# Regional attention: the score maxima reach the query tile through TensorE instead of DRAM, with a lag of one step, and the loads are issued by SyncE

## The chip, the cores and the metric

The kernel runs on one core of one Trainium2 chip. The metric is the device time of one execution in microseconds. Loading the inputs to the device is not in it.

## The reference

The input has 32 images of 56 x 56 positions with 64 channels. A 3 x 3 convolution with quantized activations (8 levels) and one-bit weights comes first, then one transformer block:

```python
xq = round(min(1, abs(x)) * 7) / 7
x  = conv3x3(xq, sign(W) * mean(abs(W))) + b
# block; 7 x 7 regions of 8 x 8 = 64 tokens, 8 heads of 8 channels
q, k, v = split(layernorm(x) @ wqkv + bqkv)
idx  = top_k(mean_region(q) @ mean_region(k).T, 4)     # 4 regions for each region
attn = softmax(q_region @ k[idx].T / sqrt(8)); o = attn @ v[idx]
x = x + o @ wo + bo
x = x + gelu(layernorm(x) @ w1 + bm1) @ w2 + bm2
```

## The kernel before, in words

The images go in 16 pairs. One **step** is one region of one image: 98 steps a pair, 1568 in all. The program's `steps` runs steps 0 to 17 once, then a loop whose body is steps 18 to 115 (`LEAD`=18, `END`=116), so that the end of one pair overlaps the start of the next. Each engine has its own instruction list, written by hand as a function `step(p, h, kind)`, and the engines meet only in semaphores. An engine does its list strictly in that order.

What a step h does, with the lags `ST_LAG`=3 and `PV_LAG`=4:

- POOL and VectorE copy the keys of the four chosen regions into `kg` (`keys`), two steps ahead; POOL copies the values into `vg`.
- TensorE, `scores` (L988): four products of `qm` and `kg`, 256 columns each, into PSUM banks 0 and 1, queries on the rows. VectorE reduces them to the maximum of each query and head (L724) into `mx`. The scores of step h+1 overwrite these banks and so wait for it.
- VectorE transposes the maxima (L731) into `tr`. SyncE (SP) writes `tr` to DRAM as `max_d` (L370) and, one step later, reads it back as one row of `qm` (L364), row 96. `kg` has -1 in that row.
- TensorE, `turned(h-3)` (L1002): the same scores again with keys on the rows, in PSUM banks 2 and 3. Row 96 subtracts the maximum in the product. ScalarE takes the exponential of each bank (L832) into `pt`.
- TensorE, `attended(h-4)` (L1019): 32 small products of `pt` and `vg`, bank 4. ScalarE copies it to `um` (L837) at the end of a group of two steps (one at the seventh).

Between these, each engine has items of two other chains, spread over the steps by tables. `p_item`: the strips of the next pair (7 strips, one every 6 steps, from step 18, offsets 0 to 10): convolution (L881, offset 0), copy to `xi` on ScalarE (L762, offset 1) and centring, square (L765, 2) and variance, normalization (3), query and key products (4), value products (L901, 5), copies of the results by VectorE (L659 and L665), and stores to DRAM. `f_item`: finishing of this pair (7 strips, one every 7 steps, from step 60, offsets 0 to 13): softmax sums (L938, 0), their reciprocal by a logarithm and an exponential (1, 2), output product (4), second normalization (5 to 7), feed-forward products L969 (9) and L974 (10), and the two products back (12, 13). At offset 10 ScalarE runs `hidden` (L813): the Gelu table is loaded, four Gelus run, and the table of the other functions is loaded back (L199). L974 there waits for VectorE's copy of the first half (`z_ready`), which stands behind the step's reduction. `x_item` is the input of the pair after the next; ScalarE takes magnitudes (L781) when an image strip has landed.

In TensorE's `step`, the order before is scores, turned, attended, then strip and finishing items. In ScalarE's it is items, the two exponentials, the copy of `um`, the loads, and last `hidden`. The loads (`loads`: queries for the next seven steps, L237, and keys and values of a half, L247) are issued from ScalarE's queue.

## Time and profile before

| | |
|---|---|
| runs, us | 5547.73, 5552.67, 5535.24; median 5547.73 |
| profiled execution: span, us | 5568.0 |
| instructions in it | 230234 |
| busy: PE, VectorE, ScalarE, POOL | 84%, 62%, 59%, 49% |
| DMA | 487.33 MB in 627124 packets |

The profile is of one execution. Its span runs from the first to the last instruction; no time of that execution outside the span is shown. In it PE is TensorE's matmul, PEld its weight load, DVE VectorE, ACT ScalarE, POOL GpSimd, SP SyncE; a q behind a name is the engine's sequencer.
### The profile page before, as it was taken

To read this page: it belongs to the slowest core of one execution; us is meant where nothing else is said; L and a number is where in the kernel's file an instruction comes from. 1 tells how busy PE (TensorE), PEld (TensorE's weight loads), DVE (VectorE), ACT (ScalarE), POOL (GpSimd) and SP (SyncE) were. 2 spreads that over 40 slices of the span, in tenths; PEclk is the share of its full clock that TensorE was granted. 3 is DMA by queue.
4 is the path that set the end of the run, shared out by engine and by line. 5 is a ranking of instruction groups with operands and counts; after the bars stand their busy time and mean duration, and the time that the engine had idled before them with its cause. 6 is when DMAs were issued, how large, how long until landed. Compare 5 with 4: busy or idle time off the path is not lost.

```text
span 5568.0 us, 230234 instructions
## 1 busy us (share of the span) xinstructions
PE 4677.0 (84%) x68754; PEld 3217.0 (58%) x68754; DVE 3447.6 (62%) x7969; ACT 3285.4 (59%) x6282; POOL 2747.0 (49%) x9656
## 2 busy tenths in 40 slices
PE   2388888888889888888888888888888888888888
PEld 1265565656556565565656656565565656556564
DVE  2266666666666666666666666666566666667665
ACT  1156556565665656556565665656556565665656
POOL 1245455454544545445454554545455454554553
PEclk8589999998998999889989999989899999989999
DMA  1333343333333333333333423333343333323311
GB/s 53 102 98 92 83 109 76 100 77 96 102 77 98 84 95 91 82 103 80 94 83 91 111 72 103 81 96 92 79 109 79 96 81 102 100 75 102 84 40 33
DMA packets 627124, 487.33 MB, mean 88 GB/s; under 512 B 483792, under 2 KB 613968, under 8 KB 615536
## 3 DMA queue, kind: packets, MB, share of 16 engines
q10 hardware_dynamic: 335360, 205.62, 16.4%
q1 hardware_dynamic: 290416, 265.73, 16.2%
q8 instruction: 603, 9.88, 0.8%
q14 instruction: 745, 6.10, 0.4%
HBM read 262.38 MB, written 208.73 MB: 85 GB/s over the span
## 4 chain that ended last, share of the span: by engine, by line
PE 45%; DMA 18%; issue 10%; SPq 7%; ACT 7%; DVE 5%; DVEq 3%; POOL 2%; ACTq 2%; POOLq 1%
DMA max_d<-tr 11%; PE ps L988 9%; PE ps L1002 7%; PE ps L1019 7%; PE ps L881 4%; DMA qm<-qk_d 3%; PE ps L938 3%; DMA xin<-in_x 3%; DVEq L223 2%; DVE mx L724 2%; SPq L327 2%; PE ps L949 2%; PE ps L901 2%; ACT hid L813 2%; PE ps L974 2%
## 5 line engine op out<-in xcount | busy, mean ns | idle before, releaser
L724 DVE TENSOR_REDUCE mx<-ps 128x4 f32<-128x1024 f32 x1568 | 1921.7, 1226 | 1702.3 <-PE ps L988 1354.0
L832 ACT ACTIVATE pt<-ps 128x512 f32<-128x512 f32 x3136 | 1694.3, 592 | 869.2 <-PE ps L1002 814.4
L506 POOL COPY vg<-vs 64x64 f32 x6272 | 1526.5, 243 | 782.0 <-POOL kg L490 576.7
L988 PE MATMUL ps<-kg,qm 96*128 96x256 f32 x6272 | 1336.2, 338 | 386.6 <-DVE mx L724 127.3
L490 POOL CAST kg<-ks 96x128 fp32r x3136 | 851.0, 297 | 1511.6 <-PE ps L1002 1156.6
L988 PEld LDWEIGHTS ps<-kg,qm 96*128 96x128 f32 x6272 | 946.8, 202 | 1053.6 <-issue 889.5
L1002 PE MATMUL ps<-qm,kg 97*128 97x256 f32 x6272 | 1119.8, 301 | 178.8 <-ACT pt L832 102.3
L1019 PE MATMUL ps<-pt,vg 128*32 128x64 f32 x50176 | 1091.4, 231 | 0.0
L1002 PEld LDWEIGHTS ps<-qm,kg 97*128 97x128 f32 x6272 | 926.2, 203 | 252.2 <-ACT pt L832 164.8
L1019 PEld LDWEIGHTS ps<-pt,vg 128*32 128x32 f32 x50176 | 826.1, 115 | 224.2 <-issue 34.8
L643 DVE CAST kg<-ks 96x128 fp32r x3136 | 625.6, 241 | 126.2 <-issue 123.5
L518 POOL TENSOR_SCALAR xin<-xin 128x448 f32<-128x448 f32 x119 | 205.1, 1723 | 449.4 <-ACT xin L781 442.6
L731 DVE STREAM_TRANSPOSE tr<-mx 128x32 f32<-128x32 f32 x1568 | 314.7, 201 | 3.4 <-issue 3.1
L881 PE MATMUL ps<-xT,wconv 128*128 128x448 bf16 x1008 | 267.6, 413 | 11.5 <-POOL xT L528 11.5
L938 PE MATMUL ps<-um,pick 128*128 128x448 f32 x448 | 213.8, 603 | 55.9 <-DVE vstg L665 40.6
L837 ACT ACTIVATE um<-ps 128x128 f32<-128x128 f32 (+1 forms) x896 | 240.5, 268 | 30.8 <-PE ps L1019 29.6
L776 ACT ACTIVATE stg<-ps,made 128x448 fp32r<-128x448 f32 x224 | 141.9, 637 | 183.1 <-PE ps L897 94.5
L974 PE MATMUL ps<-nm,w 64*128 64x448 f32 x448 | 144.0, 726 | 124.0 <-DVE hid L710 123.9
L790 ACT ACTIVATE rc<-ps 128x448 f32<-128x448 f32 x224 | 121.7, 543 | 146.6 <-PE ps L938 85.3
L762 ACT ACTIVATE xi<-ps 128x448 fp32r<-128x448 f32 x112 | 61.1, 545 | 228.3 <-PE ps L881 228.3
L781 ACT ACTIVATE xin<-xin 128x448 f32<-128x448 f32 x119 | 68.6, 576 | 207.2 <-DMA xin<-in_x 199.2
L528 POOL TENSOR_SCALAR xT<-xin 128x448 bf16<-128x448 f32 x119 | 163.1, 1371 | 28.9 <-POOL vg L506 26.2
(109 smaller groups left out, 3866.7 us busy)
## 6 DMA issues: line engine op xcount, KB each, us to landing
qk_d<-stg SPq DMA_DIRECT2D x224, 448.0 KB
qm<-qk_d ACTq DMA_DIRECT2D x1792, 42.0 KB
ks<-qk_d ACTq DMA_DIRECT2D x96, 784.0 KB, 6.2
vs<-v_d ACTq DMA_DIRECT2D x64, 784.0 KB, 6.7
xin<-in_x SPq DMA_DIRECT2D x119, 224.0 KB
xi_d<-xi SPq DMA_DIRECT2D x112, 224.0 KB
qk_d<-stg SPq DMA_DIRECT2D x112, 224.0 KB
max_d<-tr SPq DMA_DIRECT2D x1568, 2.0 KB
```

Of the source, the lines that this page charges most:

```text
L490: j = pool.tensor_copy(kg[slot][0:NP3, :, 2 + k, :], ks[place(m)[0]][0:NP3, :, bass.ds(region, 1), :].rearrange("p g o t -> p g (o t)"))
L506: j = pool.tensor_copy(dst.rearrange("p j (e x) -> p j e x", e=2)[:, :, :, 0:HD], vs[place(m)[0]][rows, bass.ds(region, 1), :].rearrange(" ...
L643: j = v.tensor_copy(kg[slot][0:NP3, :, k, :], ks[place(m)[0]][0:NP3, :, bass.ds(region, 1), :].rearrange("p g o t -> p g (o t)"))
L724: v.tensor_reduce(mx[h % 2][:].rearrange("p (g j e) -> p g j e", g=2, j=2)[:, :, :, 0], ps[:, 0:2, :].rearrange("p g (j k) -> p g j k", j= ...
L731: v.transpose(tr[h % 2][:], mx[h % 2][:]).then_inc(S["tr_ready"], 1)
L832: act.activation(pt[m % 2][:, c], ps[:, 2 + c, :], ACT.Exp, scale=float(HD) ** -0.5).then_inc(S["pt_ready"], 1)
L881: i = pe.matmul(ps[:, 5, 0:ST].rearrange("p (n y c) -> p n y c", n=NW, y=WS), wconv[:, tap, :], rhs, start=tap == 0, stop=tap == 8)
L938: pe.matmul(ps[:, 5 + i, 0:ST], pick[:], src, start=True, stop=True).then_inc(S["sum_full"], 1)
L974: pe.matmul(ps[:, (7, 5)[i], 0:ST], w1[d, 128:256], nm2[d], start=True, stop=True).then_inc(S["h_full"], 1)
L988: i = pe.matmul(ps[:, g, 256 * j:256 * j + 256], qm[c % 2][0:NP3, t, g, 2 * j:2 * j + 2, :].rearrange("p h t -> p (h t)"), kg[slot][0:NP3, ...
L1002: i = pe.matmul(ps[:, 2 + b, 256 * g:256 * g + 256], kg[slot][0:NP3 + 1, g, 2 * b:2 * b + 2, :].rearrange("p k t -> p (k t)"), qm[c % 2][0 ...
L1019: i = pe.matmul(ps[32 * j:32 * j + 32, 4, RT * u:RT * u + RT], vg[slot][:, w:w + 32], pt[m % 2][:, c, n:n + RT], start=c + e == 0, stop=c ...
```

## The change

- The maxima stay on the chip. VectorE writes them to `mx` with 66 columns for each of two head pairs; all other columns are zero. TensorE multiplies each 66-column half as weights with an identity of 128 columns (new function `shifts`), which puts the maxima as rows into PSUM bank 2, at partitions 0 and 32. ScalarE copies 2 rows x 256 from partition 0 and VectorE 2 x 256 from partition 32 into rows 96 and 97 of `qm`. The turned product contracts over 98 rows instead of 97.
- The lags are 1 (turned), 2 (attended) and 3 (copy to `um`) instead of 3, 4 and 4. `turned` waits for both copies.
- TensorE's order in a step is now: products of the maxima of step h-1, scores h, strip and finishing items, turned h-1, attended h-2. The products of the maxima wait for the first exponential of step h-2, which frees bank 2.
- ScalarE's step begins with its copy, and the copy to `um` stands before the exponentials. VectorE's step ends with its copy.
- The loads move from ScalarE's queue to SP's, and the query loads go as two at each of four steps, from the second on, instead of three, three and two at three steps. SP's two DMAs a step are gone.
- The identity lies in `hid` until that is used.

```diff
-ST_LAG = 3
-PV_LAG = 4
+KROWS = NP3 + 2
+SHW = 66
+ST_LAG = 1
+PV_LAG = 2
+UM_LAG = 3
...
         def loads(eng, p, h, kind):
-            if t in (3, 4, 5) and live((c + 1) * NW, kind):
+            if t in (2, 3, 4, 5) and live((c + 1) * NW, kind):
...
-                queries(..., [(g, h) ...][(t - 3) * 3:(t - 2) * 3])
+                queries(..., [(g, h) ...][(t - 2) * 2:(t - 1) * 2])
...
@@ sync, step @@
-                    sp.wait_ge(hopped[m % 2], (p * R + m // 2 + 1) * 16)
-                    sp.dma_start(qm[...][NP3:NP3 + 1, m % NW]..., max_d[m % RING]...).then_inc(row_ready[m % RING], 16)
-                    sp.wait_ge(S["tr_ready"], T + 1)
-                    sp.dma_start(max_d[h % RING]..., tr[h % 2][0:128:8, :]).then_inc(hopped[h % 2], 16)
+                loads(sp, p, h, kind)
...
@@ vector, step @@
-                    if live(h - 2, kind):
-                        v.wait_ge(hopped[h % 2], (p * R + (h - 2) // 2 + 1) * 16)
...
-                    v.transpose(tr[h % 2][:], mx[h % 2][:]).then_inc(S["tr_ready"], 1)
...
                     finish(p, h)
+                if live(h, kind):
+                    v.wait_ge(S["sh_full"], T + 1)
+                    v.tensor_copy(qm[h // NW % 2][NP3:KROWS, h % NW, 1]..., ps[32:34, 2, 0:256]).then_inc(S["shv_ready"], 1)
...
@@ scalar, step @@
+                m = h - ST_LAG
+                if live(m, kind):
+                    act.wait_ge(S["sh_full"], T - ST_LAG + 1)
+                    act.activation(qm[m // NW % 2][NP3:KROWS, m % NW, 0]..., ps[0:2, 2, 0:256], ACT.Copy).then_inc(S["sha_ready"], 1)
...
-                loads(act, p, h, kind)
...
@@ tensor @@
+            def shifts(p, m):
+                T = p * STEPS + m
+                pe.wait_ge(S["mx_ready"], T + 1)
+                if not (isinstance(T, int) and T == 0):
+                    pe.wait_ge(S["pt_ready"], (T - 1) * 2 + 1)
+                for j in range(2):
+                    i = pe.matmul(ps[0:SHW, 2, 128 * j:128 * j + 128], mx[m % 2][:, SHW * j:SHW * j + SHW], ident_r[:], start=True, stop=True)
+                i.then_inc(S["sh_full"], 1)
...
             def turned(p, m):
-                pe.wait_ge(row_ready[slot], (p * 14 + c + 1) * 16)
+                pe.wait_ge(S["sha_ready"], T + 1)
+                pe.wait_ge(S["shv_ready"], T + 1)
...
             def step(p, h, kind):
+                if live(h - ST_LAG, kind):
+                    shifts(p, h - ST_LAG)
                 if live(h, kind):
                     scores(p, h)
-                if live(h - ST_LAG, kind):
-                    turned(p, h - ST_LAG)
-                if live(h - PV_LAG, kind):
-                    attended(p, h - PV_LAG)
...
                     finish(p, h, kind)
+                if live(h - ST_LAG, kind):
+                    turned(p, h - ST_LAG)
+                if live(h - PV_LAG, kind):
+                    attended(p, h - PV_LAG)
```

How the change orders TensorE round a feed-forward step (finishing offset 10). Before, from the scores of that step (L988) over turned (L1002) and attended (L1019) to the feed-forward product L974:

```order
L988 MATMUL ps<-kg,qm 128x256 x3
L1000 ISA [waits row_ready4]
L1002 MATMUL ps<-qm,kg 128x256 [waits pt_ready]
L1002 MATMUL ps<-qm,kg 128x256
L1000 REGISTER_ALU
L1002 MATMUL ps<-qm,kg 128x256 [waits pt_ready]
L1002 MATMUL ps<-qm,kg 128x256
L1019 MATMUL ps<-pt,vg 32x64 [waits pt_ready,vg_ready]
L1019 MATMUL ps<-pt,vg 32x64 x15
L971 REGISTER_ALU
L974 MATMUL ps<-nm,w 128x448 [waits z_ready]
L974 MATMUL ps<-nm,w 128x448
```

Now the scores are L979, the feed-forward product L965, turned L1004, attended L1021, and the products of the maxima L991:

```order
L979 MATMUL ps<-kg,qm 128x256 x3
L962 REGISTER_ALU
L965 MATMUL ps<-nm,w 128x448 [waits z_ready]
L965 MATMUL ps<-nm,w 128x448
L1004 MATMUL ps<-qm,kg 128x256 [waits pt_ready,shv_ready,sha_ready]
L1004 MATMUL ps<-qm,kg 128x256
L1002 REGISTER_ALU
L1004 MATMUL ps<-qm,kg 128x256 [waits pt_ready]
L1004 MATMUL ps<-qm,kg 128x256
L1021 MATMUL ps<-pt,vg 32x64 [waits pt_ready,vg_ready]
L1021 MATMUL ps<-pt,vg 32x64 x15
L989 ISA [waits mx_ready]
```

The feed-forward product moved from behind the attended products to straight behind the scores, turned and attended products follow it, and the turned product waits for the two copies.

ScalarE in the same step. Before, the exponentials (L832), the copy to `um` (L837), `hidden` (L813 with its table load, L199 the table back), and the exponentials of the next step:

```order
L832 ACTIVATE pt<-ps 128x512 [waits st_full]
L831 REGISTER_ALU
L832 ACTIVATE pt<-ps 128x512 [waits st_full]
L837 ACTIVATE um<-ps 128x128 [waits u_full]
L811 ISA
L813 ACT_TABLE_LOAD
L813 ACTIVATE hid<-ps,made 128x448 [waits h_full]
L811 REGISTER_ALU
L813 ACTIVATE hid<-ps,made 128x448 [waits h_full]
L813 ACTIVATE hid<-hid,made 128x448 [waits z_ready] x2
L199 ACT_TABLE_LOAD
L831 ISA [waits u_full]
```

Now the exponentials are L830, `hidden` L801, the copy of the maxima L811, the copy to `um` L823:

```order
L829 REGISTER_ALU
L830 ACTIVATE pt<-ps 128x512 [waits st_full]
L799 ISA
L801 ACT_TABLE_LOAD
L801 ACTIVATE hid<-ps,made 128x448 [waits h_full]
L799 REGISTER_ALU
L801 ACTIVATE hid<-ps,made 128x448 [waits h_full]
L801 ACTIVATE hid<-hid,made 128x448 [waits z_ready] x2
L199 ACT_TABLE_LOAD
L810 REGISTER_ALU
L811 ACTIVATE qm<-ps 2x256 [waits sh_full]
L823 ACTIVATE um<-ps 128x128 [waits u_full]
```

The copy of the maxima of this step stands behind the table load L199, and ahead of the next exponentials.

## Rows read from the trace of the kernel before

**Rows 1.** Page: busy time of each engine; granted clock of TensorE in 40 slices.

```profile
PE 4677.0 (84%) x68754; PEld 3217.0 (58%) x68754; DVE 3447.6 (62%) x7969; ACT 3285.4 (59%) x6282; POOL 2747.0 (49%) x9656
PEclk8589999998998999889989999989899999989999
```

**Rows 2.** Windows: one pair, then stretches of it; first line names the columns.

```profile
core 0: us, PE busy (x) PEld busy (x) DVE busy (x) ACT busy (x) POOL busy (x), PEclk, DMA share, GB/s
2985.36:3313.14 327.78, 284.54 (x4297) 196.71 (x4297) 214.00 (x494) 204.62 (x392) 170.39 (x602) 0.94 0.36 93
...
3190.34:3213.82 23.48, 20.46 (x311) 13.48 (x310) 15.92 (x35) 17.63 (x33) 15.29 (x51) 1.00 0.18 49
...
3193.68:3195.80 2.12, 1.67 (x41) 1.40 (x41) 1.61 (x5) 1.37 (x4) 1.41 (x6) 1.00 0.02 5
...
3198.58:3202.84 4.26, 2.66 (x45) 1.71 (x45) 3.54 (x8) 3.68 (x7) 2.61 (x5) 1.00 0.13 44
3202.84:3205.56 2.72, 2.59 (x44) 1.46 (x42) 2.27 (x5) 2.70 (x4) 2.02 (x5) 1.00 0.01 4
3205.56:3210.33 4.77, 3.94 (x48) 2.45 (x49) 1.65 (x5) 3.10 (x7) 3.00 (x13) 1.00 0.03 5
...
3284.19:3313.14 28.95, 19.69 (x298) 13.37 (x297) 13.87 (x32) 14.38 (x26) 10.40 (x42) 0.88 0.52 117
```

**Rows 3.** Groups by shape: count | busy us, mean ns | idle before, releasers.

```profile
L724 DVE TENSOR_REDUCE mx<-ps 128x4 f32<-128x1024 f32 x1568 | 1921.7, 1226 | 1702.3 <-PE ps L988 1354.0 <-DMA max_d<-tr 346.7
...
L901 PE MATMUL ps<-wv,xh 128*128 128x128 f32 x672 | 114.0, 310 | 0.0
...
L901 PEld LDWEIGHTS ps<-wv,xh 128*128 128x128 f32 x672 | 91.3, 206 | 19.1 <-issue 10.1
...
L765 ACT ACTIVATE sq<-ps,made 128x448 f32<-128x448 f32 x112 | 81.2, 725 | 48.5 <-issue 30.7 <-PE ps L887 13.7
...
L665 DVE COPY vstg<-ps 128x384 f32<-128x384 f32 x112 | 61.3, 547 | 2.0 <-PE ps L901 1.9
...
L762 ACT ACTIVATE xi<-ps 128x448 fp32r<-128x448 f32 x112 | 61.1, 545 | 228.3 <-PE ps L881 228.3
...
L665 DVE COPY vstg<-ps 64x128 f32<-64x128 f32 x112 | 30.6, 273 | 0.0
```

**Rows 4.** Timeline round one feed-forward step: start, us, engine, what, [idle before].

```profile
3198.58 1.23 DVE L724 TENSOR_REDUCE mx<-ps 128x4 f32<-128x1024 f32 x1 [0.58 <-PE ps L988]
...
3199.36 1.07 ACT L832 ACTIVATE pt<-ps 128x512 f32<-128x512 f32 x2
...
3200.61 1.28 ACT L813 ACT_TABLE_LOAD   x1
...
3201.11 1.02 PE L974 MATMUL ps<-nm,w 64*128 64x448 f32 x4 [1.60 <-DVE hid L710]
...
3204.45 1.28 ACT L199 ACT_TABLE_LOAD   x1
...
3205.74 2.27 ACT L832 ACTIVATE pt<-ps 128x512 f32<-128x512 f32 x4
...
3206.39 0.99 PE L1002 MATMUL ps<-qm,kg 97*128 97x256 f32 x4 [0.96 <-ACT pt L832]
```

**Rows 5.** Chain that ended last, by line (page).

```profile
DMA max_d<-tr 11%; PE ps L988 9%; PE ps L1002 7%; PE ps L1019 7%; PE ps L881 4%; DMA qm<-qk_d 3%; PE ps L938 3%; DMA xin<-in_x 3%; DVEq L223 2%; DVE mx L724 2%; SPq L327 2%; PE ps L949 2%; PE ps L901 2%; ACT hid L813 2%; PE ps L974 2%
```

**Rows 6.** Waits in total: us, times, longest.

```profile
DVE mx L724 <- DMA max_d<-tr: 346.7, 193, 5.5
...
PE ps L974 <- DVE hid L710: 123.9, 108, 1.7
PE ps L988 <- DMA qm<-qk_d: 104.5, 44, 4.2
...
PE ps L1002 <- DMA qm<-max_d: 73.8, 66, 2.8
```

**Rows 7.** Line L237, the query loads: duration ns min/median/max, first and last start.

```profile
L237 ACTq DMA_DIRECT2D qm<-qk_d x1792: 304/310/1872, 222.0 to 5502.2; - x200
```

More of the change, by code:

```diff
@@ L146, in build @@
         vg = [sb(f"vg{i}", [128, 2 * VG + 8]) for i in range(RING)]
-        mx = [sb(f"mx{i}", [128, 32]) for i in range(2)]
-        tr = [sb(f"tr{i}", [128, 32]) for i in range(2)]
+        mx = [sb(f"mx{i}", [128, 2 * SHW + 2], F32R) for i in range(2)]
         pt = [sb(f"pt{i}", [128, 2, 512]) for i in range(2)]
@@ L177, in build @@
         idx_loaded = [sem(f"idx_loaded{i}") for i in range(2)]
-        hopped = [sem(f"hopped{i}") for i in range(2)]
-        row_ready = [sem(f"row_ready{i}") for i in range(RING)]
         xf_loaded = [sem(f"xf_loaded{i}") for i in range(2)]
@@ L251, in loads @@
             t, c = h % NW, h // NW
-            if t in (3, 4, 5) and live((c + 1) * NW, kind):
-                if t == 3 and not (kind == "lead" and c < 1):
+            if t in (2, 3, 4, 5) and live((c + 1) * NW, kind):
+                if t == 2 and not (kind == "lead" and c < 1):
                     eng.wait_ge(S["st_full"], (p * STEPS + c * NW) * 2)
                     settled(eng)
-                queries(eng, p + (c + 1) // 14, (c + 1) % 14, [(g, h) for g in range(NG) for h in range(HG)][(t - 3) * 3:(t - 2) * 3])
+                queries(eng, p + (c + 1) // 14, (c + 1) % 14, [(g, h) for g in range(NG) for h in range(HG)][(t - 2) * 2:(t - 1) * 2])
             if kind == "loop":
@@ L449, in _ @@
             Z = S["zero2"]
-            for i, t in enumerate((ident, pick)):
-                pool.memset(t[:], 0.0).then_inc(Z, 1)
+            for i, t in enumerate((ident, pick[:])):
+                pool.memset(t, 0.0).then_inc(Z, 1)
             pool.wait_ge(Z, 2)
-            pool.affine_select(out=ident[:], in_=ident[:], compare_op=ALU.not_equal, fill=1.0, base=0,
+            pool.affine_select(out=ident, in_=ident, compare_op=ALU.not_equal, fill=1.0, base=0,
                                pattern=[[-1, 128]], channel_multiplier=1).then_inc(Z, 1)
@@ L825, in step @@
                     finish(p, h)
+                m = h - UM_LAG
+                if live(m, kind) and group_end(m):
+                    u = 2 if m % NW % 2 else 1
+                    act.wait_ge(S["u_full"], T - UM_LAG + 1)
+                    act.activation(merged(m, u), ps[:, 4, 0:RT * u], ACT.Copy).then_inc(S["um_ready"], 1)
                 m = h - ST_LAG
```

39 lines of the change are left out of this document (12 added, 27 removed).

## The prediction

> **What bounds the kernel now.** I read the page first: TensorE is busy 84% of a span of 5568.0 us, the others 49 to 62%, and it is often granted less than full clock [rows 1]. Then I cut one pair of images into stretches. A whole pair takes 327.8 us, of which PE is busy 284.5 [rows 2]: at most 43 us a pair, about 690 us in sixteen pairs, is idle PE, and only that can be won back by removing waits. The shortest step, 2.12 us, has PE busy for 1.67 [rows 2]: it is bound by the loop maxima, scores, maxima. The reduction takes 1.23 us of it [rows 3] and the four score products with their hand-overs the other 0.89. Most other steps are bound by PE itself, because strip or finishing products fill the time of the reduction.
>
> The DMA hop of the maxima matters in some places. The chain that ended last has 11% in it, 612 us [rows 5]. VectorE waited 346.7 us for it in 193 of 1568 steps and PE 73.8 us [rows 6]. The last seven steps of a pair take 28.95 us against 23.48 for seven clean steps with no less work, and are granted 0.88 of the clock against 1.00 [rows 2]. In the clean stretch the hop costs nothing.
>
> The third thing to see is what a **feed-forward step** does to ScalarE. It loads the Gelu table, runs four Gelus and loads the old table back: from 3200.61 to 3205.74, 5.13 us with 0.27 of waiting in it, so 4.87 us of work. With a lag of three PE goes on under it, and waits only 0.96 us at the end [rows 4]. There are 112 such steps (7 strips, 16 pairs).
>
> **The change, part by part.**
>
> *The two products.* Each step gains two products of 66 weight columns and 128 moving columns, between the maxima of one step and the scores of the next. They lengthen both the PE-bound steps and the short loop. The nearest rows are the value products, 128 by 128: their weight loads take 91.3 us for 672, 0.136 each, and one product's mean is 0.310 [rows 3]. Two at 0.136 are 0.27; half as many weight columns makes it a little less, and I take **0.25 us a step, +392 us**. The lower end is half of each, 0.14 a step or 220 us. The upper is one product's whole latency and a hand-over, 0.41 or 640 us. The Trainium skill ("TensorE: Matmul & The Clock Gate", Back-to-back issue gap) gives about 81 ns a product sustained at 128 columns; by it this term would be 254 us and the time about 140 us lower. The row's 136 ns is for this data type's neighbour and these waits, so I keep to it.
>
> *The copies.* VectorE drops its transpose and copies 2 x 256 out of PSUM: between 0.273 (128 columns) and 0.547 (384) [rows 3], so about 0.41. ScalarE's 448 columns take 0.545 [rows 3], so 256 about 0.38. Both run under the scores that follow the products. VectorE's new wait (for the products of its step) holds only its next reduction, which waits for later scores anyway. On ScalarE 1568 x 0.38 = 596 us is added and the query issues are removed, 1792 x 0.310 = 556 us [rows 7]. I cost both copies at nothing; if the cover were gone they would cost up to 0.4 a step.
>
> *The lag of one, in a feed-forward step.* ScalarE's copy stands at the start of its step, behind the Gelu block of the step before; the turned product now needs that copy. Let R be the start of the reduction, 3198.58 now. The feed-forward product L974 waits for VectorE's copies behind the reduction and begins at R+2.53 [rows 4]. Now it stands straight behind the scores, and turned and attended products come after it. So: it begins at R+2.4 (no transpose), takes 1.02, the first turned bank is full at R+3.8, two exponentials of 1.07 together end at R+4.9, the Gelu block at R+9.8, the copy at R+10.2. Turned and attended products take 1.25, the next products and scores 0.25 and 0.9: the reduction two steps on begins at R+12.6. Now it begins at R+6.98 (4.26+2.72 [rows 2]). The third step takes 4.77 now with the wait of 0.96 in it; without that and with the products 4.06. Together 16.7 against 11.75: 4.9 more, 0.75 of it counted already, so 4.15. PE stands idle for over 2 and then some 4 us in it, and idle stretches are where the clock falls (0.88 in the waiting stretch [rows 2]); I add 0.7 as an estimate. **4.85 x 112 = +543 us**; ends 3.0 and 5.5, 336 and 616 us.
>
> *Finishing and strip products before the turned ones.* At strip offsets 1 and 2 PE needs a ScalarE result of the same step. ScalarE begins with the copy (0.38) and then takes 0.545 or 0.725 [rows 3]: 0.93 and 1.1 us, of which the scores, a third of the 1.67 [rows 2], cover 0.55. That is 0.4+0.55 for each of 112 strips, **+106 us** (ends 0 and 200). Steps with two ScalarE activations and no PE item are now bound by it, 0.38+1.3+1.07=2.75 against 2.37, six a pair: +38. Twice a pair PE meets a VectorE result about 1.3 us too early (routing sums, last value copy): +42. Together **+80**.
>
> *What goes.* The two DMAs a step, their issue on SP and the waits for them: 346.7+73.8 us, and with the clock lost in them more. Queries are issued a step earlier, by a queue that is not held up by activations: of 104.5 us of PE waits [rows 6] most should go. All of it adds to 525 us, but a part of VectorE's waits lies under busy PE. I take **-400 us**; ends 150, and 612+104 = 716 if the whole chain share went. The Trainium skill ("DMA: Bandwidth & Descriptors", Issuing engines are not separate DMA queues) holds that spreading DMAs over engines saves no more than issue time; by it moving the loads is worth only ScalarE's 556 us of issue, which the copies take back, and the queries' 104.5 us would stay: about 100 us more. The trace has both queues on the same engines and cannot tell it.
>
> *The sum.* 392+543+106+80-400 = +721 us on the profiled 5568.0 (span; what lies around it is not shown), so 6289. The median of the runs is 5547.7, 20 below; I take off the same and forecast **6260 us**. The start (249 us before the first maxima) and the tail stay.
>
> **Rivals.** *The hop was the bound.* Speaks for it: 11% of the chain, 28.95 against 23.48 [rows 2, 5]. If the full 716 us went, and products and Gelu steps cost their lower ends (220+336) and the waits inside a step nothing, the time is 5548-160 = about 5390: **faster**. It decides from the point where the gains pass 556 us. Against it: the clean stretch, with no hop wait, is no shorter than PE's work and its own waits, and idle PE is 690 us in all, with the feed-forward waits (123.9 [rows 6]) in it. I give 0.07.
>
> *One queue for all.* Query, key and value loads now stand in SP's queue with the image loads that ScalarE waits for. If each of 112 image strips waits as queries do now (104.5/44 = 2.4 us [rows 6]), it is +270: 6530. For it: with a lag of one a waiting ScalarE stops PE at once. Against: SP is no longer paced by every step and issues earlier. The same page of the Trainium skill (Queues, rings and completion order) says that an issuing engine's descriptors are consumed in ring order, which would make exactly this happen. Chance 0.15.
>
> *Milder.* The products cost their lower end and the Gelu steps too, gains as forecast: 220+336+106+80-400 = +342, so 5890. Chance 0.13, slower still.
>
> *The change doesn't do what it says*: the copies are not covered, since the turned product waits for VectorE's copy behind its finishing work. At 0.2 a step that is +310 on the sum, 6570. Chance 0.05, inside the range's upper end.
>
> **How the numbers follow.** My forecast's case has 0.58. The range is 5850 to 6650: it takes in the milder case and one queue, and leaves out the faster rival and both worst ends together. A measurement of this kernel tells about 0.3%. Faster 0.07, the same 0.02 (only where gains and losses cancel by chance), slower 0.91.
>
> **What would show it.** Between the maxima and the scores two products of about 0.25 us on PE; no DMA releaser of the maxima. The short step at about 2.37 us. In feed-forward steps the turned product waits some 4 us for ScalarE's copy, 112 times, and this is the longest wait of PE; the three steps take about 17 us. The last seven steps fall to about 20 us plus what the new waits add. If the feed-forward steps stay near 12 us, or the short step near 2.12, the forecast is wrong in that term; if PE's busy share rises above 90%, wholly.

## The result and the profile after

The changed kernel took 6656.12 us (median of 4, 6645.77 to 6672.94) against 5544.25 for the kernel before on the same chip: a ratio of 1.2011, with a 95% interval of 1.1976 to 1.2046. It is slower, as forecast, but by 1112 us instead of 712, and 6 us outside the range. The profiled execution's span is 6660.7 us. In one of the runs below (products only) one of four executions took 15703 us; its ratio is of the other three.

The page: busy time of each engine, TensorE's clock by slices, the DMA queue, the chain that ended last.

```profile
PE 5387.8 (81%) x71890; PEld 3664.0 (55%) x71890; DVE 3916.9 (59%) x7970; ACT 3925.9 (59%) x7850; POOL 2753.1 (41%) x9656
PEclk7798978879788897888989888898887989888898
q1 hardware_dynamic: 591280, 464.89, 27.0%
PE 55%; ACT 26%; issue 11%; DVE 3%; DVEq 2%; ACTq 1%; DMA 1%; POOL 1%; SPq 0%; POOLq 0%
PE ps L1004 11%; ACT pt L830 8%; PE ps L1021 8%; PE ps L979 8%; PE ps L872 4%; PE ps L991 4%; ACT qm L811 4%; PE ps L929 3%; ACT hid L801 3%; PE ps L940 3%; PE ps L965 2%; PE ps L950 2%; ACT L199 2%; ACT L801 2%; PE ps L960 2%
```

The maxima's DMAs have left the chain [rows 5], and ScalarE has 26% of it. PE is busy for 711 us longer [rows 1], of which the products of the maxima account for 566 at most. The granted clock has a mean of 0.859 over the span, where it was 0.909: since it has two levels, TensorE stood at the lower one for 2 x 0.141 x 6660.7 = 1878 us, before for 2 x 0.091 x 5568.0 = 1013 us. Laid over PE's busy time, the trace's record of the clock has PE at work for 1520 us at the lower level, before for 835. If work at half clock takes at most twice its time, the clock accounts for at most half the difference, 342 of the 1112 us: an estimate from these two figures, and so are the like ones below.

Groups: busy us, mean ns, and idle time before with its releaser.

```profile
L712 DVE TENSOR_REDUCE mx<-ps 128x4 fp32r<-128x1024 f32 x1568 | 1922.3, 1226 | 312.2 <-PE ps L979 178.0
L724 DVE CAST qm<-ps 2x256 fp32r<-2x256 f32 x1568 | 659.3, 420 | 2102.1 <-PE ps L991 2084.3
L1004 PE MATMUL ps<-qm,kg 98*128 98x256 f32 x6272 | 1395.2, 349 | 307.3 <-ACT qm L811 296.8
L811 ACT ACTIVATE qm<-ps 2x256 fp32r<-2x256 f32 x1568 | 583.4, 372 | 255.0 <-PE ps L991 217.5
L991 PE MATMUL ps<-ident_r,mx 128*66 128x128 f32 x3136 | 565.9, 265 | 117.3 <-ACT pt L830 59.8
L991 PEld LDWEIGHTS ps<-ident_r,mx 128*66 128x66 f32 x3136 | 332.0, 148 | 298.3 <-issue 97.6
L965 PE MATMUL ps<-nm,w 64*128 64x448 f32 x448 | 149.3, 751 | 240.1 <-DVE hid L699 240.1
```

VectorE's copy took 0.42 us and ScalarE's 0.37 (forecast 0.41 and 0.38), one weight load 148 ns. The wait of the feed-forward product for VectorE doubled, from 123.9 to 240.1 [rows 6].

Windows of one pair, in the columns of [rows 2]: a pair; seven clean steps; the short step; the three steps from a feed-forward step on; the last seven; the strip steps 1 and 2.

```profile
core 0: us, PE busy (x) PEld busy (x) DVE busy (x) ACT busy (x) POOL busy (x), PEclk, DMA share, GB/s
3539.41:3944.85 405.44, 336.94 (x4494) 229.35 (x4493) 243.28 (x494) 244.81 (x490) 170.87 (x602) 0.86 0.29 74
3773.26:3806.58 33.32, 27.56 (x322) 17.64 (x322) 17.73 (x35) 20.42 (x40) 15.69 (x53) 0.80 0.15 40
3777.56:3780.10 2.54, 2.20 (x42) 1.71 (x42) 2.00 (x4) 2.46 (x6) 1.74 (x8) 1.00 0.36 94
3783.80:3790.58 6.78, 4.59 (x48) 3.33 (x50) 3.59 (x7) 3.17 (x5) 4.60 (x8) 0.73 0.07 17
3790.58:3797.82 7.24, 5.30 (x48) 3.22 (x50) 2.59 (x5) 5.47 (x11) 4.48 (x19) 0.50 0.16 42
3797.82:3802.89 5.07, 5.07 (x50) 2.72 (x52) 1.95 (x4) 1.56 (x4) 1.49 (x6) 0.73 0.01 3
3908.95:3944.85 35.90, 25.84 (x317) 17.38 (x318) 15.91 (x32) 17.27 (x34) 11.11 (x46) 0.75 0.31 72
3639.40:3642.31 2.91, 2.32 (x43) 1.88 (x43) 2.23 (x5) 2.06 (x5) 1.52 (x7) 1.00 0.99 316
3642.31:3645.84 3.53, 2.87 (x44) 2.10 (x45) 2.00 (x4) 2.30 (x6) 1.42 (x7) 1.00 0.57 138
```

Against [rows 2], the three feed-forward steps went from 11.75 us at full clock to 19.09 at 0.73, 0.50 and 0.73. Over all feed-forward steps of the fifteen whole loop bodies the three steps have a mean of 12.61 us before and 18.83 now, so the one shown before was a short one. The short step rose by 0.42; ScalarE is busy for 2.46 of its 2.54 us. The last seven steps rose from 28.95 to 35.90.

The timeline of the same feed-forward step; the reduction R starts at 3783.80, and the counterpart is [rows 4].

```profile
3783.80 1.23 DVE L712 TENSOR_REDUCE mx<-ps 128x4 fp32r<-128x1024 f32 x1 [0.19 <-PE ps L979]
...
3785.99 1.02 PE L965 MATMUL ps<-nm,w 64*128 64x448 f32 x4 [2.23 <-DVE hid L699]
...
3786.94 1.22 PE L1004 MATMUL ps<-qm,kg 98*128 98x256 f32 x4
...
3788.87 1.28 ACT L801 ACT_TABLE_LOAD   x1
...
3792.45 1.28 ACT L199 ACT_TABLE_LOAD   x1
...
3793.75 0.37 ACT L811 ACTIVATE qm<-ps 2x256 fp32r<-2x256 f32 x1
...
3794.18 1.22 PE L1004 MATMUL ps<-qm,kg 98*128 98x256 f32 x4 [1.94 <-ACT qm L811]
...
3795.33 1.08 PE L1021 MATMUL ps<-pt,vg 128*32 128x64 f32 x32
...
3796.34 0.48 PE L991 MATMUL ps<-ident_r,mx 128*66 128x128 f32 x2
...
3796.62 1.17 PE L979 MATMUL ps<-kg,qm 96*128 96x256 f32 x4
```

The second turned product begins at R+10.4. What comes behind it is not as forecast: turned 1.22, attended 1.08, products 0.48 and scores 1.17 us, where the same lines took 0.64, 0.65, 0.34 and 0.68 at full clock (at 3601.48, 3801.41, 3801.99 and 3802.17 of the same trace). The stall was foreseen; of the half clock behind it, only 0.7 us was.

### The profile page after: what moved, and what is told of

Read it like the earlier page. It is cut to its first block, busy times and chain, and to the rows that moved or that the text cites. A ratio compares the mean times of both kernels' runs of the same rounds, so it can differ in the third digit from the quotient of the medians.

```text
span 6660.7 us, 229350 instructions
## 1 busy us (share of the span) xinstructions
PE 5387.8 (81%) x71890; PEld 3664.0 (55%) x71890; DVE 3916.9 (59%) x7970; ACT 3925.9 (59%) x7850; POOL 2753.1 (41%) x9656
## 4 chain that ended last, share of the span: by engine, by line
PE 55%; ACT 26%; issue 11%; DVE 3%; DVEq 2%; ACTq 1%; DMA 1%; POOL 1%; SPq 0%; POOLq 0%
PE ps L1004 11%; ACT pt L830 8%; PE ps L1021 8%; PE ps L979 8%; PE ps L872 4%; PE ps L991 4%; ACT qm L811 4%; PE ps L929 3%; ACT hid L801 3%; PE ps L940 3%; PE ps L965 2%; PE ps L950 2%; ACT L199 2%; ACT L801 2%; PE ps L960 2%
## 5 line engine op out<-in xcount | busy, mean ns | idle before, releaser
L830 ACT ACTIVATE pt<-ps 128x512 f32<-128x512 f32 x3136 | 1698.6, 594 | 2222.7 <-PE ps L1004 2222.7
L712 DVE TENSOR_REDUCE mx<-ps 128x4 fp32r<-128x1024 f32 x1568 | 1922.3, 1226 | 312.2 <-PE ps L979 178.0
L724 DVE CAST qm<-ps 2x256 fp32r<-2x256 f32 x1568 | 659.3, 420 | 2102.1 <-PE ps L991 2084.3
L1004 PE MATMUL ps<-qm,kg 98*128 98x256 f32 x6272 | 1395.2, 349 | 307.3 <-ACT qm L811 296.8
L1004 PEld LDWEIGHTS ps<-qm,kg 98*128 98x128 f32 x6272 | 1004.2, 212 | 1006.7 <-issue 527.6
L979 PE MATMUL ps<-kg,qm 96*128 96x256 f32 x6272 | 1206.2, 319 | 70.5 <-DVE kg L632 70.3
L1021 PE MATMUL ps<-pt,vg 128*32 128x64 f32 x50176 | 1140.5, 238 | 66.2 <-ACT um L823 62.4
L1021 PEld LDWEIGHTS ps<-pt,vg 128*32 128x32 f32 x50176 | 867.1, 120 | 307.3 <-ACT um L823 75.3
L979 PEld LDWEIGHTS ps<-kg,qm 96*128 96x128 f32 x6272 | 956.3, 213 | 74.2 <-issue 70.8
L811 ACT ACTIVATE qm<-ps 2x256 fp32r<-2x256 f32 x1568 | 583.4, 372 | 255.0 <-PE ps L991 217.5
L991 PE MATMUL ps<-ident_r,mx 128*66 128x128 f32 x3136 | 565.9, 265 | 117.3 <-ACT pt L830 59.8
L991 PEld LDWEIGHTS ps<-ident_r,mx 128*66 128x66 f32 x3136 | 332.0, 148 | 298.3 <-issue 97.6
L965 PE MATMUL ps<-nm,w 64*128 64x448 f32 x448 | 149.3, 751 | 240.1 <-DVE hid L699 240.1
L823 ACT ACTIVATE um<-ps 128x128 f32<-128x128 f32 (+1 forms) x896 | 229.0, 256 | 9.7 <-PE ps L1021 1.3
L940 PE MATMUL ps<-hid,w 128*64 128x448 f32 x448 | 187.1, 935 | 1.2 <-ACT hid L801 1.2
L965 PEld LDWEIGHTS ps<-nm,w 64*128 64x128 f32 x448 | 39.9, 217 | 265.7 <-DVE hid L699 265.7
```

What stands on the lines that cost most here:

```text
L712: v.tensor_reduce(mx[h % 2][:].rearrange("p (j w) -> p j w", j=2)[:, :, 0:64].rearrange("p j (g w) -> p g j w", w=32)[:, :, :, 0], ps[:, 0 ...
L724: v.tensor_copy(qm[h // NW % 2][NP3:KROWS, h % NW, 1].rearrange("p h t -> p (h t)"), ps[32:34, 2, 0:256]).then_inc(S["shv_ready"], 1)
L811: act.activation(qm[m // NW % 2][NP3:KROWS, m % NW, 0].rearrange("p h t -> p (h t)"), ps[0:2, 2, 0:256], ACT.Copy).then_inc(S["sha_ready"], 1)
L830: act.activation(pt[m % 2][:, c], ps[:, 2 + c, :], ACT.Exp, scale=float(HD) ** -0.5).then_inc(S["pt_ready"], 1)
L979: i = pe.matmul(ps[:, g, 256 * j:256 * j + 256], qm[c % 2][0:NP3, t, g, 2 * j:2 * j + 2, :].rearrange("p h t -> p (h t)"), kg[slot][0:NP3, ...
L991: i = pe.matmul(ps[0:SHW, 2, 128 * j:128 * j + 128], mx[m % 2][:, SHW * j:SHW * j + SHW], ident_r[:], start=True, stop=True)
```

## The experiments

Each run is given with its median and its ratio to the kernel before on the same chip. That kernel took 5536 to 5566 us on the chips used, so a difference between two kernels of different calls is taken from their ratios, times 5544 us; the change is then at 6659. Such a difference is good to some 30 us, since each ratio has an interval of about 0.0035 to either side. I first took the change apart, then built it up from the kernel without the hop, and last tried to repair it. The diffs are shortened: `...` stands for left-out code, and some lines are told in words.

**No hop in the kernel before.** The two DMAs a step and all waits for them go; the maxima are not subtracted.

```diff
-    sp.dma_start(qm[...][NP3:NP3 + 1, m % NW]..., max_d[m % RING]...)
-    sp.dma_start(max_d[h % RING]..., tr[h % 2][0:128:8, :])
-    v.wait_ge(hopped[h % 2], ...)
-    pe.wait_ge(row_ready[slot], ...)
```

> The kernel before without the hop: neither of SP's two DMAs of the maxima and no wait for them, so the maxima are not subtracted in the turned product (row 96 stays zero); all else as before, the loads on ScalarE's queue too. It prices what the change could win at most from the maxima's path. The forecast's term (400 us, most of it the hop's) expects 5130 to 5250 us. The rival by which the hop was the bound (11% of the chain, 612 us) expects 4930. If the hop was nearly hidden: 5450 or more; then the change lost more than forecast partly because there was less to win.

5296.15 us, ratio 0.9523 [0.9497, 0.9549]. The hop was worth 264 us by itself, not its 612 us share of the chain, and I had expected 5130 to 5250. ScalarE's wait for an image also fell with it, from 199.2 to 82.0 us.

**TensorE's old order in the changed kernel.**

```diff
     scores(p, h)
+    turned(p, h - ST_LAG); attended(p, h - PV_LAG)
     strip and finishing items
-    turned(p, h - ST_LAG); attended(p, h - PV_LAG)
```

> The changed kernel with TensorE's old order in a step: turned and attended products ahead of the strip and finishing items; the lag of one stays. If the order costs (feed-forward product straight behind the scores, ScalarE results wanted at once), 1.0 us at strip offsets 1 and 2 and about 1.3 at offset 10 come back: 6656-106-146, and some at other offsets: about 6350 to 6400 us. If only the lag behind the Gelu block costs, this stays within 50 of 6656. If the turned product then waits for its copies in every step, it is slower: 6800 or more.

6411.26 us, 1.152 [1.1487, 1.1553]: 272 us less than the change. The mean clock is 0.911 against 0.859. The new order costs time although the old one puts the wait for the copies straight behind the scores.

**Both copies on VectorE in the changed kernel.**

```diff
+    v.tensor_copy(qm[...][NP3:KROWS, h % NW, 0]..., ps[0:2, 2, 0:256]).then_inc(S["sha_ready"], 1)
-    act.activation(qm[...][NP3:KROWS, m % NW, 0]..., ps[0:2, 2, 0:256], ACT.Copy).then_inc(S["sha_ready"], 1)
```

> The changed kernel with both copies of the maxima on VectorE; ScalarE has none, so a turned product no longer stands behind the Gelu block of the step before, and PE goes on for one more step until the products of the maxima want an exponential. If ScalarE's copy behind the Gelu block is the cause of some 2.5 us a feed-forward step, the time falls by 112 x 2 to 3 = 220 to 340 us, to about 6370, less up to 0.2 us a step where VectorE's second copy (0.42) is not covered. If the block costs by the lag alone, whoever copies, it stays within 60 of 6656 or rises.

6465.16 us, 1.1625 [1.1595, 1.1656]: 214 us less. Its waits in total (us, times, longest):

```profile
PE ps L961 <- DVE hid L699: 276.8, 112, 2.7
...
PE ps L1017 <- ACT um L819: 201.9, 110, 3.4
PE ps L1000 <- DVE qm L724: 148.1, 275, 0.9
```

The wait for ScalarE's copy of the maxima (296.8) is gone, and the attended product now waits in 110 steps for ScalarE's copy to `um`, which stands behind the same Gelu block. So with one such wait removed the next one, behind the same block, came out.

**The products twice.**

```diff
-    for j in range(2):
+    for j in (0, 1, 0, 1):
```

> The changed kernel with the two products of the maxima done twice: the slope is the price of the pair. By the forecast's 0.25 us a step it is 392 us slower, 7050 us. If most of a pair lies under waits, under 0.1 a step: below 6820. If a pair costs its latency, 0.4: 7280.

6730.95 us, 1.2089 [1.2053, 1.2125]: the second pair costs some 43 us by the ratios and 75 by the medians, 0.03 to 0.05 a step, or 14 to 24 ns a product. That is not the price of work at a fixed clock, since the mean clock went up from 0.859 to 0.882. The Trainium skill ("TensorE: Matmul & The Clock Gate", Back-to-back issue gap) gives about 81 ns a product sustained; neither the second pair nor the first (43 ns each, below) added that much to the time.

**Lag one, no rows.** The changed kernel without the products, the copies and the waits for them.

```diff
-    shifts(p, h - ST_LAG)
-    pe.wait_ge(S["sha_ready"], T + 1)
-    pe.wait_ge(S["shv_ready"], T + 1)
-    act.activation(qm..., ps[0:2, 2, 0:256], ACT.Copy)
-    v.tensor_copy(qm..., ps[32:34, 2, 0:256])
```

> The changed kernel (lag of one, new order, loads on SP) without the products of the maxima and without both copies, so the maxima are not subtracted. Set beside the kernel before without the hop (5296 us), it differs in lag, order and loads alone; set beside the changed kernel (6656), in products, copies and their waits alone. If lag and order cost most, as the Gelu steps suggest: 6050 to 6300. If the products and the waits for the copies cost most: 5400 to 5700.

5992.62 us, 1.0827 [1.0786, 1.0869]. With nothing of the rows left, the lag and the order are slower than before by 8%, although the loads on SyncE are a gain (see below).

**Loads on SyncE in the kernel before,** hop and all.

```diff
 sync:   + loads(sp, p, h, kind)
 scalar: - loads(act, p, h, kind)
```

> The kernel before with the query, key and value loads on SP's queue, behind its two DMAs of the maxima in each step; nothing else. If one queue for all delays the maxima's hop and the image loads, it is slower, by 100 us or more. If taking 0.31 us an issue off ScalarE matters, faster by 50 to 100. By the forecast the place of the issues alone is worth at most the queries' 104 us; I expect 5480 to 5600.

6162.28 us, 1.1135 [1.1092, 1.1179]: 629 us more, where I had expected 5480 to 5600. PE's waits for queries went from 104.5 [rows 6] to 447.5, ScalarE's for an image from 199.2 to 339.6; the last two lines are what SyncE itself waited for:

```profile
PE ps L987 <- DMA qm<-qk_d: 447.5, 201, 5.1
ACT xin L783 <- DMA xin<-in_x: 339.6, 90, 8.9
...
SPq L195 <- DVE tr L733: 996.2, 715, 21.6
SPq L195 <- DMA max_d<-tr: 910.7, 658, 5.1
```

SyncE often stands still for the maxima, and the loads stand behind these waits in its list. The other way round, that the loads hold up the hop, shows less: VectorE's wait for the maxima fell from 346.7 to 200.8 us, and PE's rose from 73.8 to 134.1.

**No table loads,** in the changed kernel and in the kernel before (Gelu replaced by the identity, so that no table is switched).

```diff
-    act.activation(hid[:, i], src, ACT.Gelu_apprx_tanh, ...)
-    load_table(act)
+    act.activation(hid[:, i], src, ACT.Identity, ...)
```

> The changed kernel with the identity in place of Gelu, so neither table load is there: ScalarE's block falls from 4.9 to about 2.3 us, 2.57 less, 112 times. If the block stands on the path that sets the end in each feed-forward step: -2.4 x 112 = -270 us, and some more from the clock, 6250 to 6390. If other things set these steps: within 80 of 6656.

> The same edit in the kernel before. There PE waited 0.96 us behind the block, so 40 to 110 us less than 5548. If this falls as much as the changed kernel does, the lag of one did not put the block on the path; it was there already.

6135.31 us, 1.1085 [1.1043, 1.1128], and 5468.51 us, 0.9893 [0.9851, 0.9935]. Two table loads of 1.28 us are taken from each of 112 blocks, 2.57 us each. The changed kernel gains 513 us, 4.6 a block; the kernel before gains 59 us, 0.5 a block. That is more than the 266 to 406 us I had expected for the changed kernel. The block is on the path now and hardly was before. It costs 1.8 times its own length. The clock can be the rest: without the table loads PE is busy at the lower level for 989 us instead of 1520, worth at most 265 us beside the 288 of the loads themselves. In the strips, where no such block runs, the changed kernel's time stays the same (115.9 us a pair in both).

**Products only.** Lag one, no rows, with the products, which nobody copies (VectorE waits for them before it overwrites `mx`).

```diff
+    shifts(p, h - ST_LAG)
+    v.wait_ge(S["sh_full"], T - 1)
```

> The run with a lag of one and no rows (5993 us) plus the two products of the maxima, which nobody copies or waits for, except the reduction two steps on. It prices the first pair. By the forecast 0.25 us a step: 6385 us. By the slope of the second pair (about 70 us): 6060. What is left to the changed kernel's 6656 is the copies and the turned product's wait for them.

6147.56 us, 1.107 [1.1029, 1.111]: 135 us over the kernel without them, 0.086 a step. The pair's two matmuls have a mean of 0.265 us each, but PE's busy sum rose by only 199 us, 0.13 a step: they overlap each other and their neighbours. In the short step the pair costs more, 2.33 us against 2.12. The run lies 522 us below the changed kernel, which differs from this one by the two copies and the waits for them.

**The changed kernel with its loads on ScalarE.**

```diff
 sync:   - loads(sp, p, h, kind)
 scalar: + loads(act, p, h, kind)
```

> The changed kernel with the loads back in ScalarE's queue, behind the exponentials. Without the maxima's DMAs nothing small is behind the loads on SP, so their place should matter little: 6600 to 6700. If one queue for all costs as it did in the kernel before (626 us there), 6000 to 6300. If ScalarE's issues (0.31 us, 8 in 7 steps) stop PE at a lag of one: 6700 to 7000.

6948.31 us, 1.2506 [1.2467, 1.2545]: 274 us more. Without the hop in it, SyncE's queue is the faster one. The Trainium skill ("DMA: Bandwidth & Descriptors", Issuing engines are not separate DMA queues) holds that the choice of the issuing engine saves only issue time. This run fits that: PE's waits for queries are only 27.2 us with the loads on ScalarE, which spends 1792 x 0.31 = 556 us on issuing them, and PE's wait for ScalarE's copy grows from 109 to 206 times. The +629 us above is not issue time, which the move took off ScalarE: there the waits in SyncE's list stand ahead of the loads.

**Finishing items last,** and the same with both copies on VectorE: TensorE's order is products, scores, strip items, turned, attended, finishing.

```diff
-    finish(p, h, kind)
     turned(p, h - ST_LAG)
     attended(p, h - PV_LAG)
+    finish(p, h, kind)
```

> The changed kernel with strip items ahead of the turned products, as it has them, and finishing items behind the attended ones, as before. The full old order gave -245 us, with the strip stretch (steps 24 to 59) 6.9 us a pair slower and the rest some 23 faster. If both parts add, this keeps the second and not the first: about 6656-370 = 6290.

> The same with both copies on VectorE. If the gains add: 6290-190 = 6100 us. If VectorE's two copies behind its finishing work now hold the turned product, 6290 or more.

6322.66 us, 1.1382 [1.1349, 1.1415], and 6405.79 us, 1.1541 [1.1506, 1.1577]. This is the best version with the lag of one that still makes the rows, 349 us under the change. It is still slower than before. Moving ScalarE's copy, worth -214 in the new order, costs +88 here; why it does was not looked into.

**No hop, loads on SyncE.** The first run's kernel with the loads moved (maxima not subtracted).

```diff
 sync:   - the two DMAs of the maxima
         + loads(sp, p, h, kind)
 scalar: - loads(act, p, h, kind)
```

> The kernel before without the hop (5296 us) and with the loads on SP's queue: nothing but the place of the loads differs. In the changed kernel SP's queue was 292 us better than ScalarE's. If that gain is there at a lag of three too: about 5000 to 5200. If it is there only because a lag of one makes PE wait for whatever holds ScalarE: 5250 to 5320.

5088.16 us, 0.9165 [0.9138, 0.9193]. This is the kernel before with what the change takes away, and without what it adds: 463 us faster. PE's waits for queries are down to 25.3 us, from 81.2 without the hop alone; the move gained 199 us in all, so most of it is not in them. ScalarE's issue time is the nearest cause, not tried by itself. The page:

```profile
PE 4413.7 (87%) x68754; PEld 3073.4 (60%) x68754; DVE 3446.7 (68%) x7969; ACT 3278.3 (64%) x6282; POOL 2752.8 (54%) x9656
```

**Lag one in the old order, no rows.** The fifth run's kernel with TensorE's old order.

```diff
     scores(p, h)
+    turned(p, h - ST_LAG); attended(p, h - PV_LAG)
     strip and finishing items
-    turned(p, h - ST_LAG); attended(p, h - PV_LAG)
```

> The run with a lag of one and no rows (5993 us) in TensorE's old order. Beside e13 it differs in the lag alone, beside 5993 in the order alone. If the order behind a lag of one is the dearer part: 5500 to 5650. If the lag alone is: 5750 to 5900.

5458.20 us, 0.9821 [0.9787, 0.9855]. The page of this kernel, and under it that of the fifth run's, with the new order:

```profile
PE 4543.1 (83%) x68754; PEld 3161.0 (58%) x68754; DVE 3274.7 (60%) x6402; ACT 3271.8 (60%) x6282; POOL 2785.1 (51%) x9656
```

```profile
PE 5009.2 (83%) x68754; PEld 3356.0 (56%) x68754; DVE 3213.9 (54%) x6402; ACT 3205.2 (53%) x6282; POOL 2745.7 (46%) x9656
```

The same 68754 matmuls are busy for 4413.7 us in the run before, 4543.1 here and 5009.2 in the new order. From here to the new order the time rises by 558 us and PE's busy time by 466. The mean clocks are 0.958, 0.922 and 0.873. PE was busy at the lower level for 329, 702 and 1309 us, so the clock can account for at most 304 of the 466. The other 162 are time that the trace counts as busy at the same clock: in the strips, which ran at 1.00 in both, the sum rises by 3.7 us a pair (below). A busy sum is therefore not work alone; what else is in it was not separated.

**Rows on the chip at nearly the old lags.** Everything is computed: the lags 3, 4 and 4 of the kernel before, the old order, products with two weight columns into a free part of bank 4, one copy of 2 x 512 on VectorE, ScalarE's copy to `um` behind the exponentials again, loads on SyncE.

```diff
-ST_LAG = 1; PV_LAG = 2; UM_LAG = 3
+ST_LAG = 3; PV_LAG = 4; UM_LAG = 4
-    pe.matmul(ps[0:SHW, 2, 128 * j:...], mx[m % 2][:, SHW * j:SHW * j + SHW], ident_r[:])
+    pe.matmul(ps[0:2, 4, 128 + 128 * j:...], mx[m % 2][:, 2 * j:2 * j + 2], ident_r[:])
+    v.tensor_copy(qm[...][NP3:KROWS, h % NW]..., ps[0:2, 4, 128:384]...)
```

> A version that should beat both: the rows made on chip as in the change, but with the old lags (3 and 4) and TensorE's old order. The products write columns 128 to 383 of PSUM bank 4 instead of bank 2, with two weight columns each instead of 66, and one copy by VectorE (2 x 512) fills the rows for both head groups; the loads are on SP. From 5296 (no hop): products +155 or less, VectorE's copy 0.7 instead of the transpose's 0.2 at first covered, loads 0 to -100: 5350 to 5480, 1.5 to 3.5% faster than before. If any on-chip row costs its waits (about 508 us in the changed kernel) whatever the lag: 5700 or more.

5677.51 us, 1.0241 [1.021, 1.0273], where I had expected 5350 to 5480. Waits in total:

```profile
PEld ps L993 <- ACT um L830: 224.9, 376, 1.0
...
PE ps L993 <- ACT um L830: 129.5, 204, 0.9
```

The long waits for the Gelu block are gone: three feed-forward steps have a mean of 12.0 us. In their place the products, which now share a bank with the attended ones, wait for the copy to `um`. Against the kernel without hop and rows (5081 by ratio) this is still 596 us more. So the rows, though made in another way, cost about as much here as in the change (135 + 522), and a lag of one is not needed to make them dear.

**The same with the attended products between the two turned banks,** and the copy to `um` between the two exponentials. (The lag of `um` is the old one, 4, in both; the expectation miscalls it.)

```diff
-    turned(p, h - ST_LAG)
-    attended(p, h - PV_LAG)
+    turned(p, h - ST_LAG, 0)
+    attended(p, h - PV_LAG)
+    turned(p, h - ST_LAG, 1)
```

> The previous run's kernel (rows on the chip by two products of two weight columns, both copied by one VectorE instruction, old lags plus one for um, old order, loads on SyncE; 5677.5) with one order altered: TensorE does the attended products between the two banks of the turned product, and ScalarE copies um between its two exponentials. Nothing is left out of the computation. Theory A: the waits of the products of the maxima for the um copy (224.9 us on the weight loads, 129.5 us on the matmuls in the run before) are what the version pays above the kernel without the maxima (5088): they vanish, and the time falls by about 250 us to about 5430, 2% under the kernel before. Theory B: the 0.27 us that products and copy put into the loop of scores and maxima, and the waits of attended products for VectorE's copy, set it: the time stays at 5650 or above. Between them both have a share.

5880.30 us, 1.0609 [1.0578, 1.064]. Waits in total:

```profile
PE ps L1025 <- DVE qm L728: 109.7, 183, 1.6
...
PEld ps L996 <- ACT um L831: 78.0, 239, 0.4
```

The wait for `um` fell, and the time rose by 204 us: theory A fell. The attended products now wait for VectorE's copy. The short step is 2.38 us in it, 2.40 in the run before and 2.12 in the kernel without rows. So theory B's first half holds for the short step, but it does not account for the rise. The attended products' wait for VectorE's copy went from 60.4 to 109.7 us, also too little. Most of the rise is in PE's busy sum, from 4734.7 to 5101.9 us with the same matmuls. At most 160 us of that can be the clock (busy at the lower level for 463 and 783 us); what the rest is stays open. None of the versions that make the rows on the chip was faster than the kernel before.

## Why the prediction was wrong in size

A path from the kernel before to the changed one leads through the runs. Its steps depend on the order in which it is walked (the new order costs 558 us without the rows, 272 with them; the rows cost 657 in the new order, 942 in the old), but it has the same parts as my sum. Half clock is worked out from the mean clock as above; the last column is PE's busy time within it.

| kernel | ratio x 5544 | step | PE busy | us at half clock | PE busy there |
|---|---|---|---|---|---|
| before | 5544 | | 4677 | 1013 | 835 |
| no hop | 5280 | -264 | 4534 | 708 | 562 |
| and loads on SyncE | 5081 | -199 | 4414 | 427 | 329 |
| and lag one | 5445 | +364 | 4543 | 852 | 702 |
| and TensorE's new order | 6003 | +558 | 5009 | 1526 | 1309 |
| and the two products | 6137 | +135 | 5208 | 1387 | 1242 |
| and the copies: the change | 6659 | +522 | 5388 | 1878 | 1520 |

The step "lag one" also drops VectorE's transpose, widens the turned product by one row, puts the copy to `um` ahead of the exponentials and spreads the query loads over four steps. Where the steps lie in a pair is seen in the means of the fifteen whole loop bodies of each trace, from reduction to reduction (steps 24 to 59, with the strips; 60 to 108, with the finishing; the last seven; all 98). Single pairs differ from the mean by up to 7 us in the finishing.

| us | strips | finishing | last seven | pair |
|---|---|---|---|---|
| before | 110.0 | 175.7 | 30.0 | 333.6 |
| no hop, loads on SyncE | 97.8 | 163.2 | 24.6 | 303.3 |
| and lag one | 97.8 | 185.3 | 26.4 | 326.8 |
| and the new order | 104.0 | 207.9 | 31.5 | 362.0 |
| and the products | 106.6 | 213.0 | 32.1 | 370.8 |
| the change | 115.9 | 233.6 | 36.0 | 404.4 |

Windows of one pair each: the strips of the kernel with lag one in the old order, and strips, finishing and last seven of the same kernel in the new order:

```profile
2928.87:3026.70 97.83, 94.61 (x1586) 70.23 (x1585) 73.75 (x144) 63.82 (x129) 53.33 (x216) 1.00 0.43 120
...
3212.51:3316.57 104.06, 98.33 (x1584) 71.51 (x1582) 72.77 (x145) 61.26 (x130) 53.46 (x217) 1.00 0.40 113
3316.57:3524.97 208.40, 171.43 (x2154) 108.99 (x2155) 102.47 (x207) 114.31 (x218) 97.95 (x309) 0.85 0.29 72
3524.97:3558.06 33.09, 23.90 (x297) 16.35 (x296) 13.03 (x25) 14.03 (x27) 11.22 (x46) 0.66 0.32 75
```

In the strips the clock is full in both orders and the new one costs 6.2 us, 3.7 of them counted as busy PE. In the finishing stretch and the last seven steps the clock falls to 0.85 and 0.66.

Point by point:

- *What goes*, forecast -400, measured -463. **Right**, and the source was in part another than I thought. The gain lies in the strips (-12.3 us a pair) and in the finishing (-12.5), and least in the last seven steps (-5.4), which were to fall to about 20 and have a mean of 24.6. Seven clean steps took 23.48 us [rows 2], so little was left to win there. 263 of the 463 us are busy time of PE, at most 253 of them the clock; my limit of 690 us, all idle PE, left that out.
- *The copies*, "I cost both copies at nothing". **This is the step that failed**, and the largest single miss: +522. I had priced the turned product's wait for ScalarE's copy only behind the Gelu block (that wait is in the 543), and taken the scores as cover everywhere else. The three feed-forward steps have 1.29 us of it each, 144 in all; the other 378 us had no term. In the strip stretch, where there is no Gelu block, the copies still cost 9.3 us a pair, 0.26 a step; in the finishing stretch 20.6 us. The third run shows that moving ScalarE's copy away gives back 214 us. None of that is in the strips to speak of (115.9 to 114.8 us a pair), and PE's wait for ScalarE's copy to `um` takes its place in part. How the rest divides between VectorE's copy and the wait of the products for the exponential was not separated.
- *The lag of one, in a feed-forward step.* The mechanism was right to 0.2 us up to the start of the turned product (R+10.4 against R+10.2). **The second step that failed** is the line "I add 0.7 as an estimate" for the clock. The three steps were forecast at 16.7 us and 0.7 for the clock; the one shown takes 19.09, their mean is 18.83. In the one shown, turned, attended, products and scores ran at half clock behind the stall. Over the whole kernel the clock is worth at most 342 us against the kernel before, by the estimate above; my term was 0.7 x 112 = 78. PE is busy at half clock for 3.3 us of the three steps before and for 9.9 now.
- *Finishing and strip products before the turned ones*, forecast +80 besides the 543 and +106. Lag and order together measured 364 + 558 = 922 against a forecast of 543 + 106 + 80 = 729 (and 364 + 272 = 636 on the other path, with the rows in). The three steps have a mean of 14.49 us with lag one in the old order and 17.10 in the new, 292 of the 558 us, so nearly half of the order's price lies outside these steps.
- *The products*, forecast +392, measured +135. **Too high by about two thirds.** I took a duration from a row for a price. In the short step, which is the loop alone, the pair costs 0.21 us, near the forecast's 0.25. In the strips, where PE is nearly always busy, it costs 0.07 a step.
- The sum: -400 + 543 + 186 + 392 + 0 = 721 against -463 + 922 + 135 + 522 = 1116. The two misses that counted, the clock and the copies, were both of the kind "covered" or "small" without a row behind it. It was luck that the result lies only 6 us outside the range: the products, 257 us too dear, and the gains, 63 too small, hid 320 of a miss of 715. (The sum less 20 us is 6269; I wrote 6260.)
- By place, from the kernel without hop and rows to the change: the sum had 39.6 us a pair for the seven times three feed-forward steps, 15.6 for the strips and 15.3 for the other 41 steps; the traces have 49.7, 18.1 and 33.3. The largest part of the miss, 18 us a pair, lies in ordinary steps outside both, for which I had only the products and 5 us.
- The *rivals*. *The hop was the bound*: the gains of 463 us stayed below the 556 from which it would have decided. *One queue for all* did not happen: ScalarE's wait for an image is 81.4 us, as without the hop, and the queue gains 274 us. Where the hop stays in the same list the loads cost +629, with the images' wait at 339.6. *The copies are not covered* had a chance of 0.05 and a price of 310; it is what happened, but the wait is for ScalarE's copy, not for VectorE's.
- What was named to show it: the short step is 2.54 us, not 2.37 (2.33 with the products alone); PE's wait for ScalarE's copy is 1.94 us on the matmul and 3.40 on its weight load, not 4, 109 times, 296.8 us in all, and it is PE's longest, as said. PE's busy share is 81%.

What the level of the clock follows stays open. PE's busy share does not tell it: the finishing-last kernel is busy for 81% at a mean clock of 0.921, the one with lag one, the new order and no rows for 83% at 0.873. No run changed the clock alone, so how much of the time it made, and how much of it is only the stall's mark, can't be parted. The nearest to it is the pair of runs without table loads, where 2.57 us of stall were worth 4.6. By the estimate of 342 us above it did not make most of the loss.

## What to carry to other kernels

A lag between producer and consumer is slack for the longest item of the engine between them. Before a lag is cut, look for that item (here 4.87 us of Gelu with its tables) and for every result of that engine which the bound engine then needs in the same step; removing one such wait here exposed the next. Give no small copy a price of nothing because something else runs beside it: ask for each step what runs in front of it on its engine. Price a stall of TensorE with the matmuls behind it at half clock too. Where the busy sum of the same matmuls grows, part of the loss is there and not in the idle time, and not all of that need be the clock: compare how long PE is busy at each level. And a load is put on the engine by what that engine waits for ahead of it and by whether the engine has time to issue it.

## What the runs showed of the hardware

- The same 68754 matmuls had a busy sum of 4413.7 to 5009.2 us, with the mean granted clock falling from 0.958 to 0.873. At the same granted clock of 1.00 the sum of a strip stretch was still 94.61 in one order and 98.33 in another. More matmuls can go with a higher clock: 6272 products of the maxima instead of 3136 went with 0.882 instead of 0.859.
- A pair of products of 66 weight columns and 128 moving ones cost 0.086 us a step for the first pair and 0.03 to 0.05 for the second, where the group's mean is 0.265 for one.
- With two weight columns instead of 66 the pair takes 0.28 us from first to last instead of 0.34 (medians), and one weight load 0.083 instead of 0.138. The short step is not shorter for it: 2.40 us, and 2.33 with the products of 66 columns alone (that one has no copy in its loop).
- A table load takes 1.28 us. The Trainium skill ("ScalarE: Activation LUTs", What ACT_TABLE_LOAD costs) adds a drain that brings a switch to about 2.66 us; here the two loads and the four Gelus stand 5.13 us apart from first to last with 0.27 of waiting [rows 4], so no such drain shows beside them.
